# Spreading the gate weights inside the mixture loop, and inverting the softmax sums on GpSimd, in a graph network with mixtures of experts on Trainium2

## The reference, cut to what matters

```python
attn = jax.nn.softmax(scores, axis=-1)                      # first feed-forward layer
o = jnp.einsum('bhqk,bhkd->bhqd', attn, v)
...
p = jnp.exp(scores - m[tgt])                                # second graph layer, two times
s = jax.ops.segment_sum(p, tgt, num_segments=n)
w = p / (s[tgt] + 1e-16)
```

```python
gate = jax.nn.softmax(y @ gate_W + gate_b, axis=-1)
hid = jax.nn.gelu(jnp.einsum('bnd,edf->bnef', y, W1) + b1)
eo = jnp.einsum('bnef,efd->bned', hid, W2) + b2
out = jnp.einsum('bned,bne->bnd', eo, gate)
```

## Time and profile before

| | |
|---|---|
| median of 3 runs | 1899.19 us (1895.92 to 1900.51) |
| profiled execution, its own time | 1896.96 us |
| its span | 1895.2 us |
| busy: PE, PEld, DVE | 1602.2, 1268.2, 1272.2 us |
| busy: ACT, POOL | 902.9, 174.0 us |
| mean granted TensorE clock | 0.902 of full speed |

### The profile page before, as it was taken

How to read it: one execution, slowest core, us unless ns; L and a number is a source line. 1 busy time by engine, 2 the same in 40 slices (tenths; PEclk the granted TensorE clock), 3 DMA queues, 4 the chain that set the end, 5 groups by cost and what they waited for, 6 DMA issues and landing times. The chain is left out here.

```text
span 1895.2 us, 26037 instructions
## 1 busy us (share of the span) xinstructions
PE 1602.2 (85%) x8474; PEld 1268.2 (67%) x8474; DVE 1272.2 (67%) x2136; ACT 902.9 (48%) x1482; POOL 174.0 (9%) x135
## 2 busy tenths in 40 slices
PE   7697988998996998568989938398779999999993
PEld 6577455786774777456767734386468888888882
DVE  7853366246674476458988845624469999999993
ACT  1122144333551354116889800242148788788781
POOL 2200240001000000130000024300020000000002
PEclk9797998799998999758999969589869999999997
DMA  9001000003001001224673140000425417945002
GB/s 292 19 1 45 0 1 1 12 1 137 32 2 35 1 2 57 89 62 140 233 284 122 39 149 0 0 1 1 200 60 217 200 39 311 366 181 221 17 22 87
DMA packets 42632, 174.14 MB, mean 92 GB/s; under 512 B 10131, under 2 KB 10384, under 8 KB 27073
## 3 DMA queue, kind: packets, MB, share of 16 engines
q1 hardware_dynamic: 28702, 153.94, 21.8%
q0 software_dynamic: 8960, 10.29, 2.0%
q10 hardware_dynamic: 4896, 8.92, 1.2%
HBM read 275.74 MB, written 20.03 MB: 156 GB/s over the span
## 5 line engine op out<-in xcount | busy, mean ns | idle before, releaser
L668 PE MATMUL bank<-sb_ident,sb_XN 125*128 125x125 f32 x160 | 32.9, 385 | 95.9 <-DVE sb_XN L1614 91.6
L766 PE MATMUL bank<-sb_ident,sb_rF 125*125 125x125 f32 x520 | 85.5, 290 | 19.9 <-DVE sb_rA L1679 17.0
L734 PE MATMUL bank<-sb_W,sb_XT 128*125 128x512 f32 (+1 forms) x240 | 99.8, 571 | 1.9 <-DVE sb_XT L1583 1.5
L341 DVE TENSOR_TENSOR sb_XT_r<-sb_W,sb_XT_r 128x1024 fp32r<-128x1024 f32 x68 | 82.9, 1219 | 23.1 <-ACT sb_XT_r L1328 23.1
L668 PEld LDWEIGHTS bank<-sb_ident,sb_XN 125*128 125x128 f32 x160 | 29.5, 213 | 98.7 <-DVE sb_XN L1614 94.1
L766 PEld LDWEIGHTS bank<-sb_ident,sb_rF 125*125 125x125 f32 x520 | 66.3, 188 | 42.1 <-issue 36.3
L575 POOL TENSOR_TENSOR sb_rstd<-sb_ve,sb_half 125x5 f32<-125x5 f32 (+1 forms) x17 | 19.0, 1119 | 792.1 <-DVE sb_ve L1632 462.8
L341 DVE TENSOR_TENSOR sb_rA_r<-sb_W,sb_rA_r 128x1024 fp32r<-128x1024 f32 x68 | 83.1, 1222 | 12.1 <-ACT sb_rA_r L1328 12.1
L1240 ACT ACTIVATE sb_rF<-sb_rF,sb_nmx 125x625 f32<-125x625 f32 (+4 forms) x120 | 88.3, 738 | 2.8 <-DVE sb_nmx L1670 2.8
L341 DVE TENSOR_TENSOR sb_rB_r<-sb_W,sb_rB_r 128x1024 fp32r<-128x1024 f32 x68 | 82.8, 1218 | 0.0
L1670 DVE CUSTOM_DVE_ANT_0 sb_rF<-bank,sb_rG 125x625 f32<-125x625 f32 x80 | 61.6, 804 | 28.8 <-issue 28.8
(11 more groups left out here) (436 smaller groups left out, 4791.1 us busy)
## 6 DMA issues: line engine op xcount, KB each, us to landing
sb_W<-in_w_m SPq DMA_DIRECT2D x204, 1024.0 KB
sb_rDE<-in_w_m SPq DMA_DIRECT2D x17, 1024.0 KB
sb_rC<-slots_in SPq DMA_DIRECT2D x34, 256.0 KB, 2.8
slots_out<-sb_rC ACTq DMA_DIRECT2D x34, 256.0 KB, 2.0
sb_W<-in_w_g SPq DMA_DIRECT2D x8, 1024.0 KB, 4.9
slots_in<-sb_rC SPq DMA_DIRECT2D x1, 4608.0 KB, 14.9
sb_W<-in_w_a SPq DMA_DIRECT2D x4, 1024.0 KB, 30.6
sb_W<-in_w_m SPq DMA_DIRECT2D x2, 2048.0 KB, 18.9
```

What stands on the lines that cost most here:

```text
L341: eng.tensor_tensor(lo, src[:, HALF * h:HALF * (h + 1)], hi.bitcast(F32), ALU.subtract).then_inc(split(r, p, h, b, "lo")[0], 1)
L668: mm = pe.transpose(bank[:, t, c * R:(c + 1) * R], src[:, t, c * P:(c + 1) * P], ident[0:R, 0:R])
L734: mm = pe.matmul(bank[0:R, b, 0:cols], x[:, c, t * R:(t + 1) * R], w[:, c, 0:cols], start=(c == 0), stop=(last and c == C - 1))
L766: mm = pe.transpose(bank[0:R, 4 + kb // 4, (kb % 4) * P:(kb % 4) * P + R], SM[:, u % 4, kb * R:(kb + 1) * R], ident[0:R, 0:R])
```

## The change

There are two edits.

In the dense mixtures each unit's spread moves from ahead of the loop to just before the unit's first product, and it has bank 7 for itself; first products now use banks 5 and 6 by turns. All five sums are opened together, between the spreads of units 0 and 1. ScalarE copies a unit's spread right behind its gelu, and VectorE waits for that copy before its product.

In the attentions the addition to the sums and the inversion move from VectorE to GpSimd, as three instructions: an addition of 4 numbers, a power of -1 of 4 numbers, and a product with ones that writes 256. The semaphore `at_w` counts them.

```diff
+            def weights(base, causal):
+                c = Chain(pool, S("at_w"), base(6 * T))
+                for g in range(2 * T):
+                    t = step(4 * g, causal)[0]
+                    den, inv = dens[:, 4 * g:4 * g + 4], rden4[:, g % 2]
+                    pool.wait_ge(S("at_exp"), base(ATT) + 4 * g + 4)
+                    if g >= 2:
+                        pool.wait_ge(S("at_bc"), base(2 * T) + g - 1)
+                    c(pool.tensor_tensor(den, den, (below[:, 4:5] if causal else empty[:, t:t + 1]).broadcast_to([R, 4]), ALU.add))
+                    c.sync()
+                    c(pool.tensor_tensor(inv, den, below[:, 3:4].broadcast_to([R, 4]), ALU.pow))
+                    c.sync()
+                    c(pool.tensor_tensor(rden[:, g % 2], bcast(inv, DH), bcast(ones[0:R, 0:4], DH), ALU.mult))
...
+            weights(lambda k: 0, True)
             ln(3)
...
             with pool.Fori(0, LAYERS) as layer:
+                weights(lambda k: layer * k + k, False)
...
                 def spread(g):
-                    pe.wait_ge(S("at_norm"), base(NORM * T) + NORM // 2 * g + 2)
+                    pe.wait_ge(S("at_w"), base(6 * T) + 3 * g + 3)
...
+                if u >= 2:
+                    pe.wait_ge(S("mo_act"), UB[r] + u - 1)
...
-                        mm = pe.matmul(bank[:, 5 + u % 3, 0:n], a[:, c], b[:, c, lo:lo + n],
+                        mm = pe.matmul(bank[:, 5 + u % 2, 0:n], a[:, c], b[:, c, lo:lo + n],
...
-                open_sums(0, 3)
-                for e in range(E):
-                    for i, (lo, hi) in enumerate(HALVES):
-                        g = 2 * e + i
-                        if g >= 3:
-                            pe.wait_ge(S("rt_cb"), 2 * E * (r // 2) + g - 2)
...
+                spread(r, 0)
+                open_sums(0, T)
+                spread(r, 1)
+
+            def spread(r, u):
...
+                if u >= 1:
+                    pe.wait_ge(S("rt_cb"), 2 * E * (r // 2) + u)
+                pe.matmul(bank[:, 7, 0:n], SEL[:, e], combH[:, lo:lo + n], start=True, stop=False)
+                pe.matmul(bank[:, 7, 0:n], SEL[:, e], combL[:, lo:lo + n], start=False, stop=True).then_inc(S("rt_spread"), 1)
 
             def mixture(r):
-
-                pe.wait_ge(S("rt_cb"), 2 * E * (r // 2 + 1))
...
-                open_sums(3, T)
                 for u in range(2, UNITS + 2):
                     if u < UNITS:
+                        spread(r, u)
                         soft_first(r, u)
...
                                        bias=fvec[:, bcol + u // 2:bcol + u // 2 + 1]).then_inc(S("mo_act"), 1)
+                        act.wait_ge(S("rt_spread"), 2 * E * (r // 2) + u + 1)
+                        act.activation(CB[:, u // 2, lo:hi], bank[:, 7, 0:hi - lo], ACT.Copy).then_inc(S("rt_cb"), 1)
...
-                def weights(g):
-                    t, h, _ = step(4 * g, causal)
-                    dve.wait_ge(S("at_exp"), base(ATT) + 4 * g + 4)
-                    if g >= 2:
-                        dve.wait_ge(S("at_bc"), base(2 * T) + g - 1)
...
-                    cn(dve.reciprocal(rden[:, g % 2], bcast(den, DH)))
...
-                    if p >= 2 and p % 2 == 0:
-                        weights((p - 2) // 2)
                     if 1 <= p <= PAIRS:
                         turned(2 * p - 1)
...
-                dve.wait_ge(S("rt_cb"), 2 * E * (r // 2 + 1))
...
                         dve.wait_ge(S("mo_act"), UB[r] + u + 1)
+                        dve.wait_ge(S("rt_cb"), 2 * E * (r // 2) + u + 1)
```

More of the change, by code:

```diff
@@ L155, in graph_network @@
         half8 = sb("half8", [P, 1])
-        below = sb("below", [R, 3])
+        below = sb("below", [R, 5])
+        rden4 = sb("rden4", [R, 2, 4])
         st = sb("st", [P, 8, 6])
@@ L363, in graph_network @@
         PAIRS = ATT // 2
-        NORM = 6
+        NORM = 2
         def step(s, causal):
@@ L372, in graph_network @@
         EDGE_PREP = 4
-        CONSTS = 22
+        CONSTS = 24
         NORMS = 8 + 2 * LAYERS
@@ L551, in _ @@
             c(pool.memset(below[:, 2:3], TINY))
+            c(pool.memset(below[:, 3:4], -1.0))
+            c(pool.memset(below[:, 4:5], 1e-16))
             c(pool.memset(SELf, 0.0))
@@ L627, in _ @@
                 pool.tensor_tensor(X[:, t], X[:, t], rvec[0:R, 1], ALU.add).then_inc(S("rows_pool"), 1)
+            pool.wait_ge(S("deg_vec"), 7)
             with pool.Fori(0, LAYERS) as layer:
+                weights(lambda k: layer * k + k, False)
                 for b in range(2):
@@ L846, in router @@
                 pe.wait_ge(S("ld_b2"), 16 * (r + 1))
-                open_sums(0, 3)
-                for e in range(E):
-                    for i, (lo, hi) in enumerate(HALVES):
-                        g = 2 * e + i
-                        if g >= 3:
-                            pe.wait_ge(S("rt_cb"), 2 * E * (r // 2) + g - 2)
[L853 to L856, removed]
+                spread(r, 0)
+                open_sums(0, T)
+                spread(r, 1)
+            def spread(r, u):
+                e, i = divmod(u, 2)
+                lo, hi = HALVES[i]
+                n = hi - lo + (hi - lo) % 2
+                if u >= 1:
+                    pe.wait_ge(S("rt_cb"), 2 * E * (r // 2) + u)
+                pe.matmul(bank[:, 7, 0:n], SEL[:, e], combH[:, lo:lo + n], start=True, stop=False)
+                pe.matmul(bank[:, 7, 0:n], SEL[:, e], combL[:, lo:lo + n], start=False, stop=True).then_inc(S("rt_spread"), 1)
             def mixture(r):
-                pe.wait_ge(S("rt_cb"), 2 * E * (r // 2 + 1))
                 def second(u):
@@ L1280, in router @@
                 act.activation(combH[:, 500:N], bank[0:E, 2, 0:R], ACT.Copy).then_inc(S("rt_act"), 1)
[L1281 to L1285, removed]
             def soft_high(r, q):
@@ L1302, in mixture @@
                             act.wait_ge(S("mo_hl"), UB[r] + u - 1)
-                        act.activation(hg[:, u % 2, 0:hi - lo], bank[:, 5 + u % 3, 0:hi - lo], ACT.Gelu_apprx_tanh,
+                        act.activation(hg[:, u % 2, 0:hi - lo], bank[:, 5 + u % 2, 0:hi - lo], ACT.Gelu_apprx_tanh,
                                        bias=fvec[:, bcol + u // 2:bcol + u // 2 + 1]).then_inc(S("mo_act"), 1)
+                        act.wait_ge(S("rt_spread"), 2 * E * (r // 2) + u + 1)
+                        act.activation(CB[:, u // 2, lo:hi], bank[:, 7, 0:hi - lo], ACT.Copy).then_inc(S("rt_cb"), 1)
                     if u >= 1:
```

## The result

The changed kernel takes 1883.85 us (median of 12 runs, 1880.90 to 1888.90) beside 1898.59 us for the kernel before (12 runs). The ratio is 0.9928, with a 95% interval from 0.9912 to 0.9945: 13.7 us faster, between 10.4 and 16.7. The profiled execution took 1881.32 us, its span is 1879.6 us, 15.6 us shorter than before, and its mean clock 0.909. That lies within the range, but the sum had 21.6 us and not 13.7, so that some of its terms must be wrong.

What follows compares the result with a forecast made beforehand. TensorE was taken to set the pace in the attentions and mixture loop. Savings of 14.7 us (attentions) and 6.9 (mixtures), 21.6 in all, took the profiled 1896.96 us to 1875.4, stated as 1876; 8-in-10 range 1865 to 1886.

Steps and rivals of the forecast that it cites:

- the sum: Whole kernel: 14.7 us saved in the attentions plus 6.9 in both mixtures, 21.6 us in all.
- The attention terms: Attentions: TensorE's waits for VectorE's copy vanish; 8.4 us in two layers, 6.0 in the causal one, 0.3 at its tail.
- the cousin of rival (a): End of the causal attention: with shorter TensorE waits the clock may hold longer, for a microsecond or two; no separate chance.
- rival (a): Mixture starts: clock stays at 2.4 GHz, about 8 us saved per mixture, 9 more in all, 1867; chance 0.17.
- GpSimd's chain: Attentions: three GpSimd instructions take 2.0 to 2.2 us a group, at most 3.7, hidden; thinnest cover about 2.5 us.
- Rival (b): Attentions: GpSimd holds VectorE up some 2 us a group, TensorE's waits stay, the 14.7 us are gone, 1890; chance 0.08.
- The start of a mixture: Before unit 2's first product: moving 13 of 16 spreads away saves 7.2 and 7.3 us in the two mixtures.
- The fall that I let stand: Mixture starts: the clock drops at the same moment as before, about 359.3 and 1236.5, during products with 8 rows.
- The loop: Mixture loop: 13 spreads at 0.29 us add 3.8 us a mixture; waits for copies add nothing.
- the prediction's own sign: Mixtures: the prediction called itself wrong if their gain was above 6 or below 0 us each.
- Rival (c): Mixture loop: copies come late and TensorE waits 0.5 us at each spread, 6.5 us a mixture, 1889; chance 0.10.
- Rival (d): Mixture loop: the clock falls inside it, doubling its work's time; about 1925 with a whole loop low; chance 0.05.

Runs made afterwards that it cites:

- attention_alone: Kernel before plus only the attention edit, mixtures unchanged: median 1878.25 us, ratio 0.9891 (0.9864 to 0.9918) to the kernel before.
- mixture_alone: Kernel before plus only the mixture edit, attentions unchanged: median 1898.84 us, ratio 1.0002 (0.9986 to 1.0019) to the kernel before.
- all_128_rows: Changed kernel with operands of spreads and opened sums 128 rows high instead of 8, added rows zero: 1868.47 us, ratio 0.9857 to the kernel before.
- spread_twice: Changed kernel with each spread's two matmuls issued a second time for units 2 to 15: 1892.27 us, ratio 0.9978 to the kernel before.

## Why the prediction came out as it did

**The attention terms (14.7 us).** Right in mechanism, too small. From the first scores to the last weighing the causal attention went from 72.9 to 65.0 us, 7.9 for 6.3, and each layer's from 88.2 to 83.7, 4.5 for 4.2. In the causal one part of the surplus is, by these readings, the clock. Before, it fell already at 314.47 to 316.47 (0.60), some 7 us before the last weighing at 322.47; after, at the last weighing, 315.05. That is the cousin of rival (a), and the microseconds were lost again soon after. The kernel after (columns as in the earlier trace rows; the last two stretches hold most of the gate's products):

```profile
315.05:317.05 2.00, 1.11 (x6) 0.48 (x6) 0.00 (x1) 0.38 (x1) 0.66 (x2) 0.58 0.00 0
321.05:323.05 2.00, 2.00 (x6) 1.25 (x6) 0.00 (x0) 0.41 (x2) 0.00 (x0) 0.72 0.00 0
337.05:339.05 2.00, 1.39 (x13) 1.39 (x13) 1.41 (x2) 1.59 (x4) 0.00 (x0) 1.00 0.47 168
339.05:341.05 2.00, 2.00 (x12) 2.00 (x12) 0.00 (x0) 0.00 (x0) 0.00 (x0) 0.55 0.31 102
```

The clock comes back by 323 and falls again within the 40 gate products, which have 8 columns each and took 7.1 us in the place of 4.5. Before, it fell in the attention and then behind the gate:

```profile
314.47:316.47 2.00, 1.94 (x12) 1.03 (x12) 1.88 (x8) 1.55 (x8) 0.00 (x0) 0.60 0.03 8
...
346.47:348.47 2.00, 2.00 (x21) 2.00 (x20) 0.00 (x0) 0.00 (x0) 0.00 (x0) 1.00 0.10 31
348.47:350.47 2.00, 0.52 (x5) 0.43 (x4) 1.00 (x6) 0.24 (x1) 0.00 (x0) 0.64 0.00 0
```

From the last weighing to the router's turn after and attention_alone take 31.4 us, and the nine other kernels with an attention edit 31.0 to 31.5; before and mixture_alone take 28.2 and 28.4. So some 3 us are lost wherever the attention edit is, 3.2 in the changed kernel. The earlier fall also lets the clock rise earlier and stay up longer behind it, which gave back 1.0 us in the first products of units 0 and 1 and shortened the start in the first mixture, 7.3 us beside 9.5 in mixture_alone. No experiment shifted this fall by itself, so that the tie between the two falls is argued, not shown.

**GpSimd's chain (2.0 to 2.2 us, nothing lost).** The size is right: 2.0 us, additions of 0.2, powers of 1.0, products of 0.61 for my 0.75. Where the cover was thinnest TensorE did wait, 0.36 us once, against the forecast: my 2.5 us of cover were read at a clock of 0.50, and at full clock the last group had 1.75 (from 313.74 to 315.49). Rival (b) falls: the waits that it would have kept are gone. The masks of 625 keys beside the first chain of a layer, at 486.58 and 487.32, took 0.81 and 0.80 us, as without it, and a group's last product 0.41 us in both kernels. By the Trainium skill's rule (SBUF — State Buffer, "Who interferes with whom") these, with one input in SBUF each, were not to be held up, and the trace agrees.

**The start of a mixture (7.25 us saved).** Nearly right at an equal clock history: 6.7 and 6.5 us in mixture_alone. The fall that I let stand came. Its reason, products of 8 rows, I held only as a remark against rival (a); all_128_rows shows that it decides: with 128 rows in the same products the clock stays at 1.00. (The Trainium skill, TensorE: Matmul & The Clock Gate, "What's actually happening", ties the clock to how busy TensorE has been. With the same instructions and the same columns the clock depended on the rows in use: it was 0.50 with TensorE busy 4.00 of 4.00 us and 1.00 with it busy 5.58 of 6.05 us, so that busy time in the profile does not tell it.)

**The loop (3.8 us added a mixture).** This step failed: "13 spreads at 0.29, 3.8 us, in full". The 0.29 was read from a row of spreads, each behind another of its own height, and there it is right, as spread_twice shows. Between products of 128 rows a pair costs 0.67 us: 13 x 0.67 = 8.7 us, 4.9 more in each mixture, 9.8 in both. An expert was to be 0.5 to 0.6 us longer and is 1.34 us longer. Each mixture came out 2.3 us slower in mixture_alone, and 0.4 and 2.1 us slower with both edits, not 3.45 faster. By the prediction's own sign (a gain below 0 in a mixture) its account of the mixtures was wrong. I had priced the columns and the waits but not the switch. Rival (c), the late copies, has the right size (0.5 us for each of 13) and the wrong cause: between 384 and 420 us TensorE's matmuls wait once, 0.5 us for VectorE (L1957), and never for ScalarE's copy, and the exposed load vanishes with 128 rows while the copies stay. Rival (d) falls, the clock in the loop is 1.00.

**The sum.** 17.0 us in the attentions, 3.2 given back at the gate, 1.1 won in the first products of units 0 and 1, 2.5 lost in the mixtures (0.4 and 2.1) make 12.4 us; the other 3.2 us of the 15.6 between the two spans lie in stretches that no edit touches, and the ratio says 13.7. The forecast of 1876 lay 7.9 us too low. In the trace the 12.4 us are 9.2 fewer than the sum's 21.6. The loops took 10.3 us more than their terms (from a start's end to the mixture's end 9.3 and 8.7 us were added for 3.8 each) and the gate 3.2, against 2.3 us that the attentions, 1.1 that the first products and 0.9 that the starts gave above their terms. That the time lay in the range is in part luck: errors of opposite sign kept it there, and the 12.4 us alone would have made 1886, the range's edge.

## What to carry to other kernels

Price a matmul by its neighbours. Between products of another height (rows of contraction) it costs its columns and two exposed weight loads, here 0.39 us a pair; padding the small operand with zero rows to 128 costs no time on TensorE and takes that away. The attentions' scores have 64 rows between products of 125; whether they pay the same, no run here asked. And before a small product is moved or counted, look at the clock around it: a stretch of small heights ran at half the clock here, and zero rows up to 128 kept it at full speed. VectorE's inversion is charged by the numbers it goes through: invert first, spread afterwards.

## What the runs showed of the hardware that was not expected

- A weight load of 8, 32 or 64 rows is not hidden beside a matmul of 128 rows, nor one of 128 beside one of 8 (0.28 us from the first product to the second where 0.17 is usual); between equal heights it is.
- In the opened sums and spreads the granted clock followed the rows in use: it fell to 0.50 where the opened sums had 8 rows and stayed at 1.00 where all had 128, in six starts of three kernels.
- VectorE's inversion costs 6.25 ns a number (178 ns for 4, 1753 ns for 256), GpSimd's power of 4 numbers 1.0 us.
- Stretches some 20 us apart can be tied by the clock: in all eleven kernels with an attention edit the 8 us won in the causal attention came with some 3 us lost behind it, in and around the gate. What ties them is argued, not shown.
